# Writing out the image loop of a deformable convolution, and subtracting the low parts of every second tile on GpSimd

## The reference, cut to what matters

```python
offset = clip(conv(x, off_w, off_b), -8, 8)
mask   = 2 * sigmoid(conv(x, mask_w, mask_b))
# for each of the 9 taps and each pixel: four corners of the shifted place,
# weighted bilinearly and by the mask
p = corner(y0, x0) + corner(y0, x0 + 1) + corner(y0 + 1, x0) + corner(y0 + 1, x0 + 1)
y = einsum("bckhw,ock->bohw", p, w) + b
x = x + gelu(batch_norm(y))
```

## Time and profile before

| what | value |
|---|---|
| median of 3 runs | 3529.34 us (3527.95 to 3532.04) |
| profiled execution, its own time | 3531.29 us |
| its span, first to last instruction | 3529.4 us |
| mean granted TensorE clock | 0.961 of full speed |
| TensorE matmul / weight load busy | 3229.3 us (91%) / 2274.4 us (64%) |
| VectorE busy | 2692.8 us (76%) |
| ScalarE busy | 2439.1 us (69%) |
| GpSimd busy | 1468.7 us (42%) |

### The profile page before, as it was taken

The page is one execution under the profiler, slowest core; times in us unless marked ns, Lnnn a source line. Parts: engine busy times, 40 slices in busy tenths (PEclk is TensorE's granted clock), DMA queues, the critical chain, the costliest instruction groups (busy, mean ns, idle before and its releaser), DMA issues. The chain is left out here.

```text
span 3529.4 us, 64576 instructions
## 1 busy us (share of the span) xinstructions
PE 3229.3 (91%) x20030; PEld 2274.4 (64%) x20030; DVE 2692.8 (76%) x5130; ACT 2439.1 (69%) x5999; POOL 1468.7 (42%) x1536
## 2 busy tenths in 40 slices
PE   7989999999999999769999999968988989888887
PEld 3468878787787888658888888734444444444443
DVE  4588889888888988668888888736777677677775
ACT  4456666666666666647777777728878778777784
POOL 2245545454444555432222222221255454453535
PEclk9999999999999999889999999968999999999997
DMA  7699999999999999720000000022223222322221
GB/s 284 237 386 388 387 365 392 354 389 359 383 374 352 382 362 381 277 75 16 18 18 16 18 16 18 18 77 66 58 82 94 64 79 67 92 74 67 57 71 51
DMA packets 216833, 640.97 MB, mean 182 GB/s; under 512 B 31232, under 2 KB 111104, under 8 KB 216192
## 3 DMA queue, kind: packets, MB, share of 16 engines
q0 software_dynamic: 82944, 453.02, 33.3%
q1 hardware_dynamic: 133632, 184.79, 16.3%
HBM read 529.65 MB, written 62.62 MB: 168 GB/s over the span
## 5 line engine op out<-in xcount | busy, mean ns | idle before, releaser
L2062 DVE TENSOR_REDUCE e_neg_top<-e_next 128x1 f32<-128x1024 f32 x384 | 469.7, 1224 | 196.0 <-PE e_next L2375 168.3
L519 DVE SCALAR_TENSOR_TENSOR b_mix<-b_got,b_weight,b_mix 128x384 f32<-128x384 f32 x864 | 528.1, 618 | 89.3 <-ACT b_mix L603 47.6
L519 DVE SCALAR_TENSOR_TENSOR b_mix<-shared,b_weight,b_mix 128x384 f32<-128x384 f32 x864 | 528.5, 618 | 80.2 <-ACT b_mix L603 58.6
L615 ACT ACTIVATE b_s_high<-b_bank 128x384 fp32r<-128x384 f32 x576 | 283.7, 493 | 405.8 <-PE b_bank L725 405.8
L2229 ACT ACTIVATE e_prob<-e_s 128x512 f32<-128x512 f32 x768 | 416.6, 598 | 126.2 <-PE e_s L2387 124.8
L2214 ACT ACTIVATE e_unused<-e_next,e_neg_top 128x1024 bf16<-128x1024 f32 x384 | 430.5, 1121 | 102.4 <-DVE e_neg_top L2062 102.4
L402 POOL DMA_INDIRECT b_got<-pair_table,b_index x288 | 309.2, 1074 | 320.2 <-DVE b_mix L519 248.3
L402 POOL DMA_INDIRECT shared<-pair_table,b_index x288 | 307.4, 1067 | 310.9 <-DVE b_mix L519 243.5
L1282 ACT ACTIVATE d_w_qkv<-d_back,d_neg_top 128x128 f32<-128x128 f32 x768 | 269.7, 392 | 143.4 <-DVE d_neg_top L1185 143.4
L748 PE MATMUL b_bank<-b_s_high,b_w_high 128*128 128x512 f32 x1296 | 357.2, 403 | 0.0
L748 PE MATMUL b_bank<-b_s_high,b_w_low 128*128 128x512 f32 x1296 | 348.7, 395 | 0.0
(11 more groups left out here) (243 smaller groups left out, 6449.8 us busy)
## 6 DMA issues: line engine op xcount, KB each, us to landing
pair_table<-kept SPq DMA_DIRECT2D x16, 1536.0 KB, 13.3
e_stack<-e_high SPq DMA_DIRECT2D x384, 64.0 KB, 2.0
shared<-in_x SPq DMA_DIRECT2D x8, 1536.0 KB, 7.6
shared<-in_x SPq DMA_DIRECT2D x16, 768.0 KB, 12.2
tokens<-y SPq DMA_DIRECT2D x64, 192.0 KB, 1.9
e_tok<-tokens SPq DMA_DIRECT2D x8, 1536.0 KB, 7.5
e_stack<-e_low SPq DMA_DIRECT2D x192, 64.0 KB, 2.0
shared<-tokens SPq DMA_DIRECT2D x8, 1536.0 KB, 7.2
```

The source lines that it names most:

```text
L519: ins = nc.vector.scalar_tensor_tensor(dst[:], src[:, q * C:(q + 1) * C], weight[g][:, q, k, i:i + 1], dst[:], ALU.mult, ALU.add)
L615: nc.scalar.activation(here(s_high, s, i), tps[t % 2][:, 0:C].rearrange("p (o q) -> p o q", q=P), ACT.Copy).then_inc(highs_made, 1)
L2062: nc.vector.reduce_max(neg_top[s % 2][:, t:t + 1], b_next[t % 2][:], AX.X, negate=True).then_inc(top_ready, 1)
```

## The change

Two things change. The four Fori loops over images are replaced by Python loops, so that each image has instructions of its own and all waits compare with constants. And in each step of four tiles the tiles 1 and 3 (i odd) get their low part in another way: `take_high` is left out; ScalarE's `low` copies the whole value from the bank into `s_full`, which lies at the same place as `s_low`; and GpSimd subtracts `s_high` from it in SBUF, in place. GpSimd does this for the tile BEHIND = SLOTS + 3 = 11 back, in front of the gather of an even tile. The semaphore `counted` is replaced by further counts of `fchain`. TensorE gets two waits: for all four high parts of a step before its first product, and for GpSimd's two low parts of the step before the low products.

```diff
+    BEHIND = SLOTS + 3
+        low_at = nc.sbuf_base
         s_low = [sb(mem, f"b_s_low{u}", [CH, WIDE], F32R) for u in range(2)]
+        s_full = [sb_at(f"b_s_full{u}", [CH, WIDE], F32, low_at + 4 * u * CH * WIDE) for u in range(2)]
...
+                def low(n, t):
+                    s, i = divmod(t, GROUP)
+                    pool.wait_ge(lows_made, TURN * n + t + 3)
+                    pool.nop(nofuse=True)
+                    part = slice(i * P, (i + 1) * P)
+                    nc.gpsimd.tensor_tensor(s_low[s % 2][:, :, part], s_full[s % 2][:, :, part],
+                                            s_high[s % 2][:, :, part], ALU.subtract).then_inc(pool_lows, 1)
                 def gather(n, first=False):
                     for t in range(TURN):
+                        behind = TURN * n + t - BEHIND
+                        if behind >= 0 and behind % 2:
+                            low(*divmod(behind, TURN))
...
-                with pool.Fori(1, BATCH) as n:
+                for n in range(1, BATCH):
                     gather(n)
+                for t in range(TURN - BEHIND, TURN):
+                    if t % 2:
+                        low(LAST, t)
...
-                with dve.Fori(1, SPILLED) as n:
-                    blends(n)
-                blends(SPILLED, this=False)
-                for n in range(SPILLED + 1, BATCH):
-                    blends(n, before=False, this=False)
+                for n in range(1, BATCH):
+                    blends(n, before=(n <= SPILLED), this=(n < SPILLED))
...
                 def low(n, t):
-                    act.wait_ge(high_taken, TURN * n + t + 1)
+                    if i % 2:
+                        ins = nc.scalar.activation(here(s_full, s, i), tps[t % 2][:, 0:C].rearrange(
+                            "p (o q) -> p o q", q=P), ACT.Copy)
+                        ins.then_inc(lows_made, 1)
+                        return
+                    act.wait_ge(high_taken, (TURN * n + t) // 2 + 1)
...
                 def take_high(n, t):
                     s, i = divmod(t, GROUP)
+                    if i % 2:
+                        return
...
                 def product(n, s, i):
+                    if i == 0:
+                        pe.wait_ge(highs_made, GROUP * (STEPS * n + s + 1))
...
                         if j == 2 * CH * CH:
-                            pe.wait_ge(lows_made, GROUP * (STEPS * n + s + 1) + 2)
+                            pe.wait_ge(lows_made, GROUP * (STEPS * n + s + 1) + 1)
+                            pe.wait_ge(pool_lows, 2 * (STEPS * n + s + 1))
...
-                with pe.Fori(1, BATCH) as n:
+                for n in range(1, BATCH):
                     turn(n)
```

More of the change, by code:

```diff
@@ L271, in offsets_and_conv @@
         high_taken = sem("b_high_taken")
+        pool_lows = sem("b_pool_lows")
         lows_made = sem("b_lows_made")
@@ L274, in offsets_and_conv @@
         acc_ready = sem("b_acc_ready")
-        counted = sem("b_counted")
         y_staged = sem("b_y_staged")
@@ L528, in count @@
                     src = staged if spilled else kept[:, 2 * (n - SPILLED) + g]
-                    ins = nc.vector.bn_stats(conv_stats[:, o, bass.ds(2 * n + g, 1)], src[:, o])
+                    ins = nc.vector.bn_stats(conv_stats[:, o, 2 * n + g:2 * n + g + 1], src[:, o])
                     if o == CH - 1:
-                        ins.then_inc(counted, 1)
+                        ins.then_inc(fchain, 1)
                 def blends(n, start=0, first=False, before=True, this=True):
@@ L627, in take @@
                     act.wait_ge(acc_ready, 2 * n + g + 1)
-                    if spilled and not (isinstance(n, int) and n == 0 and g == 0):
+                    if spilled and not (n == 0 and g == 0):
                         act.wait_ge(y_spilled, 32 * n + 16 * g)
-                        act.wait_ge(counted, 2 * n + g)
+                        act.wait_ge(fchain, 8 * BATCH + 2 * n + g)
                     dst = staged if spilled else kept[:, 2 * (n - SPILLED) + g]
@@ L667, in _ @@
                 turn(0, first=True)
[L668 to L672, removed]
+                for n in range(1, BATCH):
+                    turn(n, is_last=(n == LAST), before=(n <= SPILLED), this=(n < SPILLED))
                 low(LAST, TURN - 1)
@@ L739, in product @@
                     g, k = divmod(s, TAPS)
-                    if i == 0 and k == 0 and not (isinstance(n, int) and n == 0):
+                    if i == 0:
+                        pe.wait_ge(highs_made, GROUP * (STEPS * n + s + 1))
+                    if i == 0 and k == 0 and not (n == 0):
                         pe.wait_ge(y_staged, 2 * n + g - 1)
```

## The result

The changed kernel takes 3673.69 us (median of 4 runs, 3670.61 to 3676.08) against 3530.69 us for the kernel before: ratio 1.0403, 95% interval 1.0385 to 1.0421. It is slower, as forecast, but by 143 us where 41 were forecast, and just outside the range.

What follows compares the result with a forecast made beforehand. TensorE was taken to bound the kernel before, VectorE after. Sixteen halves going from 75.3 to 80.1 us (+76), edges -36.8 and first tiles +2 made +41, about 3570 us; range 3530 to 3670 us, held at 0.8.

Steps and rivals of the forecast that it cites:

- The mechanism: In the blend, GpSimd's SBUF subtractions hold VectorE's two-SBUF-input instructions, about one in six, making VectorE the bound; chance 0.6.
- the edges: TensorE's stalls where the Fori loops over images turn; six cost 36.8 us together, and writing the loops out removes them.
- VectorE's own half of 68.0 us: VectorE's time for half an image when not held up: 36 tiles of 1.84 us and three counts of 0.59 us.
- the size of one term: VectorE's loss for each GpSimd subtraction: 0.67 us, 18 per half, 12.1 us a half.
- the upper bound: VectorE loses all 0.99 us of GpSimd's instruction at each subtraction: a half of 85.8 us, about 3662 us.
- `take_high`: On TensorE, each of the 288 `take_high` left out saves 0.18 to 0.26 us.
- DMAs: DMA queues limited to 393 GB/s, so the 29.1 MB of a half need at least 74.1 us.
- GpSimd as a bound: Rival, with a heavier hold: GpSimd needs up to 5.0 us for two tiles, a half of 90 us, 3729 us; chance 0.2.
- TensorE's wait for GpSimd's low parts: TensorE's new wait in each step before the low products: nothing charged, as TensorE has 1.1 us of slack per step.
- The no-hold rival: GpSimd's reads do not stop VectorE's blend: 3474 us, or 3417 us without a DMA limit; chance 0.15.

Runs made afterwards that it cites:

- copy: Changed kernel, but GpSimd copies the 384 elements in place with tensor_copy, one SBUF input, the subtraction left out: 3519.54 us.
- behind the gather: Changed kernel, but GpSimd subtracts after the gather of the even tile instead of in front of it: 3682.11 us.
- half the size: Changed kernel, but GpSimd subtracts only 64 of the 128 pixels of a tile, the rest of these low parts left out: 3551.31 us.
- another moment: Changed kernel, but GpSimd starts each subtraction only after one more wait, for the tile 8 back to be mixed: 3553.60 us.
- the run with the memset: Changed kernel, but GpSimd writes 1152 zeros to a buffer nobody reads where it subtracted, the subtraction left out: 3442.10 us.
- the two runs without the hold: Changed kernel with bn_stats (one SBUF input) for three blend instructions on VectorE, 3442.54 us; and with a GpSimd memset instead of the subtraction, 3442.10 us.

## Why the prediction was right and wrong

The mechanism was right: VectorE became the bound because GpSimd's reads hold it, it loses one instruction in six, the edges are gone, TensorE waits for `b_mix`, and the time is longer. VectorE's own half of 68.0 us stands; 68.0 + 18 x 1.05 = 86.9 is the measured half.

The step that failed is the size of one term: "I take 0.67 because it was measured with instructions that follow closely on each other, as here." It measured 1.03 to 1.05 us. 16 x 18 x (1.05 - 0.67) = 109 us is all of the miss of 104 us; the edges gave back 3 us more than forecast. The reading behind it, "GpSimd gets in between two VectorE instructions that follow on each other", is true of the earlier trace rows and of the run with one more wait, not of the changed kernel. There GpSimd starts when VectorE's instruction has been recorded as started for 0.2 to 0.3 us and holds up that very one. In both cases VectorE's instruction ends 0.41 to 0.43 us after GpSimd's: so do all 286 lengthened ones of the changed kernel, and 1981 of 1997 in the eight runs in which GpSimd reads. Of the 16 others 14 are in the run with the copy; there both engines' instructions are lengthened and VectorE's ends first. From this one relation follows: loss = length of GpSimd's instruction - 0.2 us + the time by which it starts after VectorE's (0.62 us of its own, 0.42 of them after the hold). The lines shown above, with GpSimd's length and start taken without its own wait:

| run | GpSimd's length | starts after VectorE's | loss by the relation | loss in the lines |
|---|---|---|---|---|
| changed kernel | 1.03 | +0.26 | 1.09 | 1.72 - 0.62 = 1.10 |
| behind the gather | 1.03 | +0.27 | 1.10 | 1.72 - 0.62 = 1.10 |
| half the size | 0.60 | +0.26 | 0.66 | 1.28 - 0.62 = 0.66 |
| copy | 0.52 | +0.24 | 0.56 | 1.18 - 0.62 = 0.56 |
| another moment | 1.00 (1.23 less a wait of 0.23) | 701.05 - 701.21 = -0.16 | 0.64 | 1.25 - 0.62 = 0.63 |

The earlier trace rows hold the same relation. I read a price from them, and not how it comes about.

What was given as the upper bound, the whole length of GpSimd's instruction, is about what happened, and even it was a little low: 0.99 us, a half of 85.8 us and 3662 us in all, against 1.05 us, 86.85 and 3674. By the relation the loss is more than the whole length when GpSimd starts more than 0.2 us after VectorE. The Trainium skill, page "SBUF — State Buffer", section "Who interferes with whom", says that issue order decides who blocks, and that the loser blocks fully. The runs agree that one of the two is blocked, and with one more wait the other order came about. But by the recorded starts the rule of the Trainium skill doesn't come out: in the changed kernel VectorE's instruction starts first and is the one that is held. And one whole instruction of GpSimd's would be 0.99 us, where the runs show 0.6 to 1.1 for the same subtraction, by the moment.

The other terms. Edges: -36.8 forecast, -40 measured. `take_high`: 0.18 to 0.26 us forecast, 0.175 measured; it didn't matter with VectorE as the bound. DMAs: 74.1 us a half as a limit was wrong; in the run with the memset they deliver a half in 72.05 us, at 406 GB/s in one window. GpSimd as a bound: the changed kernel has it busy 59.9 us of 87, and the memset shows that its load is no limit even at 72 us a half. TensorE's wait for GpSimd's low parts was 7 us in all of 1200, where nothing was charged. The no-hold rival gave 3417 to 3474 us; the two runs without the hold took 3442 us.

## What to carry to other kernels

Before work is moved to GpSimd, look what VectorE does meanwhile: beside VectorE instructions with two SBUF inputs each subtraction of 1.02 us on GpSimd cost VectorE 0.6 to 1.1 us here, and VectorE did the same work for 0.48. When two engines meet again and again in a loop, they can lock into one phase: at 243 of the 288 subtractions of the changed kernel GpSimd starts 0.24 to 0.34 us after a tile's first blend instruction, which is then held. So a price read from one meeting is a price for that phase: work out the relation of starts, ask which phase the loop will settle in, and try one more wait. What a removed stall is worth depends on the bound (40 us or 13 us here), so cost such edits in the state that the other edits leave.

## What the runs showed of the hardware

In the changed kernel a GpSimd instruction that starts 0.26 us after a VectorE instruction goes first and does not wait (1.03 us). With the one wait more, it also starts 0.26 us after (700.82 against 700.56), and there it waits and VectorE's is left alone. So the recorded starts alone don't say who wins. What tells the two cases apart in the traces is when GpSimd's sequencer was through with the wait ahead of the subtraction (line 393). That instruction at the two meetings, the changed kernel first (duration in ns, then its start in us):

```profile
L393 POOLq EVENT_SEMAPHORE  x1: 17/17/17, 701.0 to 701.0; - x1
```

```profile
L393 POOLq EVENT_SEMAPHORE  x1: 43/43/43, 700.7 to 700.7; - x1
```

The wait was over 1.4 us before the subtraction's start in the changed kernel, and 0.1 us before it in the other. In the eight runs in which GpSimd reads, 1473 instructions of the blend that were under way when GpSimd's started were held while GpSimd's kept its length, and at 1470 of these meetings the wait had been over for 0.59 us or more. At all 364 meetings at which GpSimd's instruction waited instead, it had been over for less than 0.2 us. (In the three others GpSimd's starts less than 0.05 us after VectorE's.) So the one wait more changed the outcome without changing the recorded distance of the starts. What the engine does between the end of the wait and its recorded start, no run shows.

A copy by GpSimd with one input (0.52 us) holds VectorE as a subtraction does, a memset of 1.08 us does not. `count`, which has one SBUF input, takes its 0.69 us also at the 15 places where it meets a subtraction in the changed kernel. The DMA queues moved 406 GB/s in a window of 70 us with the memset, where the most in any such window of the kernel before is about 400.
